# A graph network kernel: 84 tiles of edge records written row by row from two DMA queues during gather passes, and gathers without a loop

## What is computed

```python
message = table[src]                                   # one row per edge
out = segment_sum(weight * message, dst, num_segments=n)
```

## Time and profile before

| | us |
|---|---|
| median of the runs | 9,854.47 |
| the profiled execution, its own time | 9,853.46 |
| its span, first to last instruction | 9,851.7 |
| GpSimd (POOL) busy | 7,073.0 |
| TensorE (PE) busy | 6,580.5 |
| VectorE (DVE) busy | 5,043.2 |
| ScalarE (ACT) busy | 1,313.1 |

### The profile page before, as it was taken

How to read it: one execution, slowest core, us unless ns; L and a number is a source line. 1 busy time by engine, 2 the same in 40 slices (tenths; PEclk the granted TensorE clock), 3 DMA queues, 4 the chain that set the end, 5 groups by cost and what they waited for, 6 DMA issues and landing times. The chain is left out here.

```text
span 9851.7 us, 143700 instructions
## 1 busy us (share of the span) xinstructions
PE 6580.5 (67%) x30272; PEld 5016.5 (51%) x30272; DVE 5043.2 (51%) x16370; ACT 1313.1 (13%) x3288; POOL 7073.0 (72%) x8234
## 2 busy tenths in 40 slices
PE   2777755666688888841888856666566667876665
PEld 1656643333566664521777734444455556743333
DVE  7676654443455542665777734444422225744445
ACT  0000000000000002730000010000222225720000
POOL 1777777777777777776777777777377776737775
PEclk9666555555655668555999975555677778975555
DMA  1211112222333332001777742332366665532222
GB/s 52 52 46 49 48 29 58 52 52 52 92 104 104 104 99 87 5 11 29 220 220 219 219 107 56 60 60 55 93 185 185 185 185 140 151 119 52 52 52 53
DMA packets 663097, 934.86 MB, mean 95 GB/s; under 512 B 278665, under 2 KB 441076, under 8 KB 662636
## 3 DMA queue, kind: packets, MB, share of 16 engines
q0 software_dynamic: 273312, 613.35, 23.6%
q1 hardware_dynamic: 389708, 320.66, 11.2%
HBM read 790.44 MB, written 143.03 MB: 95 GB/s over the span
## 5 line engine op out<-in xcount | busy, mean ns | idle before, releaser
L784 PE MATMUL sage_window<-sage_hot,sage_message 128*128 128x128 f32 x4992 | 1479.4, 437 | 664.7 <-DMA sage_message<-t_x,sage_index_stage 321.0
L784 PE MATMUL block_window<-block_hot,block_message 128*128 128x128 f32 x3328 | 1196.1, 460 | 721.2 <-DMA block_message<-t_rel,block_index_stage 335.0
L784 PEld LDWEIGHTS sage_window<-sage_hot,sage_message 128*128 128x128 f32 x4992 | 1100.3, 299 | 1043.8 <-issue 728.8
L784 PEld LDWEIGHTS block_window<-block_hot,block_message 128*128 128x128 f32 x3328 | 796.5, 297 | 1093.2 <-issue 618.0
L699 DVE TENSOR_TENSOR first_acc<-first_acc,sage_window 128x128 f32 (+1 forms) x1664 | 591.6, 356 | 982.3 <-PE sage_window L784 979.0
L596 POOL DMA_INDIRECT block_message<-in_x,block_index_stage x832 | 853.8, 1026 | 237.5 <-issue 222.0
L1965 POOL DMA_INDIRECT eh_message<-t_q,eh_stage x880 | 832.1, 946 | 251.9 <-issue 232.5
L784 PE MATMUL gat_window<-gat_hot,gat_message 128*128 128x128 f32 x6656 | 849.7, 281 | 183.7 <-DVE gat_hot L604 93.2
L596 POOL DMA_INDIRECT gat_message<-t_h,gat_index_stage x832 | 793.3, 953 | 237.5 <-issue 222.0
L596 POOL DMA_INDIRECT sage_message<-t_s,sage_index_stage x832 | 789.0, 948 | 237.5 <-issue 222.1
L596 POOL DMA_INDIRECT rgcn_message<-t_rel,rgcn_index_stage x832 | 788.7, 948 | 237.5 <-issue 222.1
(11 more groups left out here) (485 smaller groups left out, 10839.6 us busy)
## 6 DMA issues: line engine op xcount, KB each, us to landing
eh_window<-t_p SPq DMA_DIRECT2D x880, 64.0 KB
t_hidden<-eh_hidden SPq DMA_DIRECT2D x110, 512.0 KB, 3.0
sc_rows<-t_hidden SPq DMA_DIRECT2D x110, 512.0 KB, 3.6
eh_low_rows<-t_low SPq DMA_DIRECT2D x110, 256.0 KB, 3.5
t_rel<-n_h SPq DMA_DIRECT2D x49, 512.0 KB, 2.6
eh_message<-t_q,eh_stage POOLq DMA_INDIRECT x880
block_message<-in_x,block_index_stage POOLq DMA_INDIRECT x832, 2.5
sage_message<-t_x,sage_index_stage POOLq DMA_INDIRECT x832, 2.5
```

Of the source, the lines that this page charges most:

```text
L784: last = nc.tensor.matmul(ps[k][:, b, :], message[u][:, f:f + P], hot[:, u, j * P:(j + 1) * P], start=(j == 0), stop=(j == heads - 1))
```

## The change

There are three parts.

1. The gathers of all seven passes are written out one by one instead of in a loop. Each reads its index from its own column of the wide table (`index[:, it*U+u]`), so the `stage` tiles, ScalarE's copies and the carrier go. GpSimd waits for `half_used` itself (in `edge_hidden` for `made`, by quarters).
2. 84 of the 122 tiles of records that `after_gat` wrote move into three passes, 28 each: sage1, sage2 and gat. In each pass SyncE writes 14 tiles and ScalarE 14. They load the tiles' records, and then, partition by partition, 14 places into registers (`queued_places`) and issue 14 DMAs of one record (16 bytes) each, 1,792 DMAs per queue and pass. At the end each waits for all of its DMAs.
3. `after_gat` writes 38 tiles of records instead of 122.

SyncE's new function stands in the block behind those it had.

```diff
+QREC = 14
+QUEUED = {name: T - (k + 1) * 2 * QREC for k, name in enumerate(("sage1", "sage2", "gat"))}
-PLACED["gat"] = (sum(n for _, n in PLACES), T - sum(n for _, n in PLACES))
+PLACED["gat"] = (sum(n for _, n in PLACES), min(QUEUED.values()) - sum(n for _, n in PLACES))
...
+def queued_places(nc, m, p, t0, engine):
+    return nc.values_load_multi_w_load_instructions(
+        m.position[p:p + 1, t0:t0 + QREC], engines=[engine], min_val=0, max_val=DUMP + 2 * P - 1,
...
-        @block.scalar
-        def _(act):
-            with act.Fori(0, ITERS, 1) as it:
-                for h in range(2):
-                    act.wait_ge(e.half_used[h], half0 + it)
-                    nc.scalar.copy(stage[h][:], index[:, bass.ds(it * U + h * HU, HU)]).then_inc(e.staged, 1)
+        if queued:
+            @block.sync
+            def _(sp):
+                t0 = QUEUED[queued]
+                sp.dma_start(rows[:, 0:QREC], m.t_rec_dst[:, t0 * REC:(t0 + QREC) * REC].rearrange("p (t k) -> p t k", k=REC)).then_inc(rows_in_sp, 16)
+                sp.wait_ge(rows_in_sp, 16)
+                for p in range(P):
+                    at = queued_places(nc, m, p, t0, SP)
+                    for j in range(QREC):
+                        sp.dma_start(m.t_rec[bass.ds(at[j], 1), :], rows[p:p + 1, j, :]).then_inc(put_sp[p % 2], 16)
+                for k in range(2):
+                    sp.wait_ge(put_sp[k], 16 * QREC * P // 2)
+            @block.scalar
+            def _(act):
...                                                     # the same with tiles t0 + QREC on, on ScalarE's queue
         @block.gpsimd
         def _(pool):
-            with pool.Fori(0, ITERS, 1) as it:
+            for it in range(ITERS):
                 for u in range(U):
                     h, k = divmod(u, HU)
-                    if k == 0:
-                        pool.wait_ge(e.carried, staged0 + it * 2 + h)
-                        pool.wait_ge(e.staged, staged0 + it * 2 + h + 1)
-                        nc.gpsimd.tensor_tensor(m.carrier[:], m.ones_i[:], m.ones_i[:], ALU.add).then_inc(e.carried, 1)
+                    if k == 0 and half0 + it > 0:
+                        pool.wait_ge(e.half_used[h], half0 + it)
                     pool.indirect_dma_start(message[u][:], None, table,
-                                            bass.IndirectOffsetOnAxis(ap=stage[h][:, k:k + 1], axis=0)).then_inc(e.gathered[u], 16)
+                                            bass.IndirectOffsetOnAxis(ap=index[:, it * U + u:it * U + u + 1], axis=0)).then_inc(e.gathered[u], 16)
...
-            with pool.Fori(0, ITERS2, 1) as it:         # edge_hidden
+            for it in range(ITERS2):
                 for u in range(U):
-                    ...                                 # carrier as above
+                    if u % QU == 0 and it >= 1:
+                        pool.wait_ge(made[u // QU], it)
                     pool.indirect_dma_start(message[:, u, :], None, m.t_q,
-                                            bass.IndirectOffsetOnAxis(ap=stage[h][:, k:k + 1], axis=0)).then_inc(gathered[u // QU], 16)
+                                            bass.IndirectOffsetOnAxis(ap=m.dst[:, it * U + u:it * U + u + 1], axis=0)).then_inc(gathered[u // QU], 16)
...
-                aggregate(nc, m, "sage1", m.t_x, m.src, [], 1, clears_tables=True, loads=w.loads)
+                aggregate(nc, m, "sage1", m.t_x, m.src, [], 1, clears_tables=True, loads=w.loads, queued="sage1")
-            aggregate(nc, m, "sage2", m.t_s1, m.src, [], 2, loads=w.loads)
+            aggregate(nc, m, "sage2", m.t_s1, m.src, [], 2, loads=w.loads, queued="sage2")
-            aggregate(nc, m, "gat", m.t_h, m.src, [m.alpha[:, 0], m.alpha[:, 1]], 2, own=True)
+            aggregate(nc, m, "gat", m.t_h, m.src, [m.alpha[:, 0], m.alpha[:, 1]], 2, own=True, queued="gat")
```

More of the change, by code:

```diff
@@ L25 @@
 SP = mybir.EngineType.SP
+ACTIVATION = mybir.EngineType.Activation
 P = 128
@@ L490, in bases @@
         skip_runtime_bounds_check_because="a first destination is a node, or NODES in the padding; a block's first source is a node")[1]
+def queued_places(nc, m, p, t0, engine):
+    return nc.values_load_multi_w_load_instructions(
+        m.position[p:p + 1, t0:t0 + QREC], engines=[engine], min_val=0, max_val=DUMP + 2 * P - 1,
+        skip_runtime_bounds_check_because="an edge's place lies in the order by source, or in the rows behind it")[1]
 def clear_tables(nc, m, sp, zeros, zeros_ready, written):
@@ L505, in fill_records, with aggregate @@
     sp.wait_ge(written, 16)
-def aggregate(nc, m, phase, table, index, weights, blocks, clear=True, degree=False, clears_tables=False, places_edges=False, own=False, fuses=None, loads=(), orders=False):
+def aggregate(nc, m, phase, table, index, weights, blocks, clear=True, degree=False, clears_tables=False, places_edges=False, own=False, fuses=None, loads=(), orders=False, queued=None):
     e = m.edge
@@ L520, in aggregate @@
     hots0, e.hots = e.hots, e.hots + (T + HU) * heads
-    half0, done0, used0, staged0 = n * ITERS, n * ITERS * (U - 2), n * T, n * 2 * ITERS
+    half0, done0, used0 = n * ITERS, n * ITERS * (U - 2), n * T
     with ExitStack() as ctx:
@@ L525, in aggregate @@
         hot = sb("hot", [P, U, heads * P])
-        stage = [sb(f"index_stage{h}", [P, HU], I32) for h in range(2)]
         ps = [pb(f"window{k}", [P, outs, P]) for k in range(HU)]
@@ L541, in aggregate @@
         weights_in = sem("weights_in")
+        if queued:
+            rows, (rows_in_sp, rows_in_act) = sb("queued", [P, 2 * QREC, REC]), sem("queued_in_sp", "queued_in_act")
+            put_sp, put_act = ([sem(f"put_{n}{k}") for k in range(2)] for n in ("sp", "act"))
         block = ctx.enter_context(nc.Block())
@@ L575, in _ @@
                 fill_records(nc, m, sp, blank, zeros_ready, written)
-        @block.scalar
-        def _(act):
-            with act.Fori(0, ITERS, 1) as it:
-                for h in range(2):
-                    act.wait_ge(e.half_used[h], half0 + it)
-                    nc.scalar.copy(stage[h][:], index[:, bass.ds(it * U + h * HU, HU)]).then_inc(e.staged, 1)
+        if queued:
+            @block.sync
[11 more added lines that the diff above has]
+            def _(act):
+                t0 = QUEUED[queued] + QREC
+                act.dma_start(rows[:, QREC:2 * QREC], m.t_rec_dst[:, t0 * REC:(t0 + QREC) * REC].rearrange("p (t k) -> p t k", k=REC)).then_inc(rows_in_act, 16)
+                act.wait_ge(rows_in_act, 16)
+                for p in range(P):
+                    at = queued_places(nc, m, p, t0, ACTIVATION)
+                    for j in range(QREC):
+                        act.dma_start(m.t_rec[bass.ds(at[j], 1), :], rows[p:p + 1, QREC + j, :]).then_inc(put_act[p % 2], 16)
+                for k in range(2):
+                    act.wait_ge(put_act[k], 16 * QREC * P // 2)
@@ L1913, in edge_hidden @@
         message = sb("message", [P, U, C])
-        stage = [sb(f"stage{h}", [P, HU], I32) for h in range(2)]
         low_rows = sb("low_rows", [P, 2, HU * P], BF16)
@@ L1921, in edge_hidden @@
             [sem(f"{n}{q}") for q in range(QUADS)] for n in ("gathered", "made", "hot_ready", "taken", "squared"))
-        attr_in, low_in, stored, staged = ([sem(f"{n}{h}") for h in range(2)] for n in ("attr_in", "low_in", "stored", "staged"))
+        attr_in, low_in, stored = ([sem(f"{n}{h}") for h in range(2)] for n in ("attr_in", "low_in", "stored"))
         window_in = [sem(f"window_in{q}") for q in range(QUADS)]
-        carried, w_in, cleared = sem("carried", "w_in", "cleared")
+        w_in, cleared = sem("w_in", "cleared")
         block = ctx.enter_context(nc.Block())
@@ L1956, in _ @@
         def _(pool):
-            with pool.Fori(0, ITERS2, 1) as it:
+            for it in range(ITERS2):
                 for u in range(U):
[L1959 to L1964, removed]
+                    if u % QU == 0 and it >= 1:
+                        pool.wait_ge(made[u // QU], it)
                     pool.indirect_dma_start(message[:, u, :], None, m.t_q,
-                                            bass.IndirectOffsetOnAxis(ap=stage[h][:, k:k + 1], axis=0)).then_inc(gathered[u // QU], 16)
+                                            bass.IndirectOffsetOnAxis(ap=m.dst[:, it * U + u:it * U + u + 1], axis=0)).then_inc(gathered[u // QU], 16)
         @block.scalar
         def _(act):
-            def stage_indices(it, h):
-                nc.scalar.copy(stage[h][:], m.dst[:, bass.ds(it * U + h * HU, HU)]).then_inc(staged[h], 1)
             def take(it, q):
@@ L1979, in take @@
                 nc.scalar.activation(square[:, q % 2], ps[q][:], ACT.Square, accum_out=m.moments[:, 1, bass.ds(n, 1)]).then_inc(squared[q], 1)
-            for h in range(2):
-                stage_indices(0, h)
-            with act.Fori(0, ITERS2 - 1, 1) as it:
+            with act.Fori(0, ITERS2, 1) as it:
                 for q in range(QUADS):
                     take(it, q)
```

3 lines of the change are left out of this document (1 added, 2 removed).

## The result

| | median of the runs (us) | lowest to highest |
|---|---|---|
| before, beside it on the same chip | 9,855.17 | 9,854.09 to 9,856.15 (4) |
| changed | 10,869.52 | 10,867.94 to 10,873.58 (4) |

The changed kernel takes 1.103 times as long (95% interval 1.1011 to 1.1049). The forecast was 10,527 us with a range up to 10,870: the sign is right and so is the main place (gat), the size is short by 343 us, and the result lies at the very end of the range. Some three quarters of the 343 us lie in the two sage passes, where the forecast had 5 us less each.

The account below looks back on a forecast made before the run. GpSimd's gather pitch was taken to bound the passes, and its 122 records the stretch behind gat. 9,853.5 + 772.3 - 59 - 40.5 = 10,526.3, with the median's 1.0 10,527 us; range 10,350 to 10,870.

Parts of the forecast that it names:

- I take 1.0, the middle: Queue parts in sage1, sage2, gat: a load of 14 registers costs 1.0 us, between 0.73 and 1.28.
- ScalarE ... I give it SyncE's price: ScalarE's queue part, without DMAs in the old trace, was priced like SyncE's: 863 us a pass.
- hidden up to 1.2 times my price: ScalarE's part starts with each pass and stays hidden beside it up to 1.2 times the 863 us.
- gat, +772.3 us forecast: SyncE's 863 us part starts behind its own-row loop in gat and ends the block at 6,483 against 5,710.7.
- One DMA 0.41: Queue parts: one 16-byte DMA with a register address costs 0.41 us, bounds 0.30 and 0.517.
- The stretch behind gat, -59 us: With 38 records instead of 122, TensorE's chain and SyncE's stores end the stretch: 63 us gained, less 4.
- The 4 us charged for a cold clock: Stretch behind gat: TensorE, idle before, was expected to start at a lower clock, costing 4 us.
- Written-out gathers, -40.5 us: Gathers without carrier outside gat: 5 passes x 5.1, edge pass 10, first gathers 5, together 40.5 us.
- A: Rival: queues dearer, 1,090 us a part, gat +999.5 and sage passes +59 each, 10,882 us; chance 0.11.
- The load by the register, named under A: Skill's rule of about 200 ns per register, 14 registers 2.8 us, a part 1,093 us; 0.03 of A's 0.11.
- B: Rival: every small store stalls its queue, 2,150 us a part, gat +2,060, sage +1,120 each, about 14,060; chance 0.03.
- C: Rival: SyncE's part goes out between own-row loads and does not end gat; 9,750 us; chance 0.05.

Follow-up runs that it names:

- e5: Changed kernel with ScalarE's queue taking 12 tiles a pass instead of 14, the rest going to GpSimd behind gat: 10,965.12 us, ratio 1.1113 to the kernel before.
- e11: Kernel without record queues, plus last-pass register loads of several lengths and first columns, on SyncE, then on ScalarE alone: 9,797.36 us, ratio 0.994.
- e9: Changed kernel with ScalarE's load beginning two columns earlier and two values longer, the same 14 DMAs following: 10,591.02 us, ratio 1.0747 to the kernel before.
- e6: Changed kernel with SyncE's gat partitions issued between its 49 loads of own rows instead of behind them: 10,145.95 us, ratio 1.0285 to the kernel before.
- e12: Changed kernel with only the written-out gathers, no record queues, the 84 tiles staying behind gat; e1 on the result's chip: 9,796.9 us, ratio 0.9941.
- e8: Kernel without record queues, plus last-pass loads of 1 to 14 values from column 0, on SyncE, then on ScalarE alone: 9,817.41 us, ratio 0.995.
- e10: Changed kernel with all queue loads on the boundary, 16-tile queues (SyncE 12 interleaved in gat), fewer GpSimd places elsewhere: 9,699.06 us, ratio 0.9841.
- e1: Changed kernel with written-out gathers but no record queues, 84 tiles staying behind gat, on the slower chip: 11,953.91 us, ratio 0.9791 to the kernel before.

## Why the prediction was wrong in size

- **"I take 1.0, the middle", for the load of 14 registers.** This is the step that failed, with the next one, which hung on it. The row on which it rests (8 in 0.69) was taken as a price by the register, between no growth and proportion. It was 1.46 on SyncE, above my upper bound of 1.28, and 3.4 on ScalarE. Two things were not known: 14 is three groups of four and two single values, and ScalarE's 14 begin at column 818. Both stand in the diff (QREC = 14, and the columns T - 28 and T - 28 + 14), but the kernel before has no register load of another size than eight.
- **"ScalarE ... I give it SyncE's price", "hidden up to 1.2 times my price".** The price of a DMA carried over (0.389 beside 0.407). The load did not, for a reason that lies in the first column and, but for 4 to 6%, not in the engine (e5, e11). ScalarE's part was 1,162 to 1,176 us, up to 1.36 times my 863, so both sage passes overran: +133.9 and +127.0 us where the sum had nothing but the gathers' -5 each. e9 takes this away by alignment alone. In gat it is covered by SyncE's part (6,072.4 against 6,813.9), and comes into view once that is moved (e6).
- **gat, +772.3 us forecast, +847.2 measured.** The mechanism was right: SyncE's part stands behind the loop of 49 own rows and ends the block. Moved in between, it is gone (e6, gat 1,170.5). A partition took 938.6/128 = 7.33 us and not 6.74: 0.46 from the load, 0.17 from what stands round it, -0.04 from the 14 DMAs. That is 75 of the 75 us.
- **One DMA 0.41.** Right: 0.407 from start to start.
- **The stretch behind gat, -59 us.** Measured -63.6. TensorE's 196 matmuls run from 6,820.5 to 6,907.0, 86.5 us after an idle 861.9; before they took 85.9. The 4 us charged for a cold clock were not paid: TensorE was granted 0.52 in the first 5 us (6,820 to 6,825) and 1.00 from then on, but before it had started alike, with 0.63 in its first 5 us (5,716 to 5,721) and then 1.00. The end stays TensorE's chain and SyncE's small stores, as argued; GpSimd's 38 records start until 6,866.0:
```profile
L1696 PE MATMUL n_ps<-n_wrel,second_acc x196: 592/592/1192, 6820.5 to 6906.4; 128*128 128x512 f32 x196
...
L844 POOL DMA_INDIRECT t_rec<-n_records,all_position x38: 965/969/1003, 6818.8 to 6866.0; - x38
```
- **Written-out gathers, -40.5 us.** Measured alone -57.5 (e12); by pass 5.5, 6.7, 10.9, 9.3, 7.5, 8.9 and 6.8 us. The pitch in e12 is 1.249 to 1.251 in five passes, as taken, 1.261 in gat and 1.341 in block0 (before 1.271 and 1.346); sage1, sage2, gat, rgcn and block3 gave more than the 5 to 6 taken, sage2 and gat most, block0 about that, and the edge pass 8.9 instead of 10 to 11.
- **Rivals.** A's number (10,882) is 12 us from the result, and that is luck, as is the result's place just inside the range, whose upper end was drawn almost at A. In A's sum gat grows by 999.5 us and the sage passes by 59 each; measured are 847 and 134 and 127, so two errors cancel. One half of its mechanism came: a queue's part too long for its cover in the sage passes, though it was ScalarE's and not SyncE's. Its reason, small DMAs behind big ones, was wrong: they kept 224 ns in gat. The load by the register, named under A, was right for ScalarE only. The Trainium skill (Runtime: NRT & Kernel Launch, Instruction fetch mechanics) gives about 200 ns per register. Off a 16-byte boundary e11 agrees (0.20 per value, and 0.30 once); on it the runs show 0.056 per value in whole groups of four, and there the measurement decides. By 200 ns I should have charged ScalarE 2.8 to 3.1, and I set the rule aside because of the one row that I had, 0.69 for 8; that row begins on the boundary. B did not come: the longest of SyncE's DMAs is 316 ns, of ScalarE's 877. C did not come as the kernel stands; e6 is C made true for SyncE's part by another order; gat then ends with ScalarE's.

The measured differences of the blocks account for the whole: 9,853.5 + 847 + 134 + 127 - 64 - 24 (gathers outside the sage passes and gat) = 10,873.5, beside this execution's 10,873.6 (the highest of the four). This is a tally of lengths; that the load is the cause is shown by e9, where ScalarE's load begins at another column, with two more values and everything else as it was, and 277 us leave the two sage passes.

## What to carry to other kernels

A price taken from one row holds for the shape and the address of that row: before it is scaled, ask in which units the cost grows and where the operand begins. Loads of registers should begin on a 16-byte boundary and take whole groups of four, even if some values go unused. When an instruction is dearer on one engine than on another, change where its operand begins before the engine is blamed. Work written behind a loop that waits for another engine starts only when that engine is done; put a piece into each turn of the loop, and see that the piece is shorter than the turn.

## What the runs showed of the hardware

- A register load of 14 values costs 1.4 us from a column divisible by four and 3.1 to 3.2 from any other, on both queues; 16 cost 1.2 and 3.5 to 3.6 (e8, e11).
- Small DMAs with a register address go out 0.407 us apart on SyncE and 0.383 to 0.389 on ScalarE, and thousands of them beside a pass leave the gathers' pitch as it is (sage1 1,044.1 us without, 1,044.5 with 4,096 in e10).
- One chip ran the kernels 22 to 24% slower (before 12,222.82 us, e1 and e12 are the same kernel with 11,953.91 and 9,796.9); there single register instructions of a queue took up to 1.4 us instead of 0.04, and the queue parts lost most. Why was not tested.
